# Two transformer blocks and a router: the second block's tiles cut across sequences, its attention moved to TensorE

## What is computed

```python
x  = x + xattn(layernorm(x), ctx)          # cross-attention, 16 heads of 32, 77 context rows per sequence, causal
h  = layernorm(x)                          # input of the second block, called with S = 8, B = 512
l1 = layer_norm(h) * ln1w + ln1b
q, k, v = split(l1 @ qkv_weight.T)         # 16 query heads, 4 key/value heads of 32
# einsum('bgqsd,bgtd->bgqst'): for each of the 512 positions, attention over the 8 SEQUENCES, causal in the sequence
h1 = h + attention(q, k, v) @ proj_weight.T
l2 = layer_norm(h1) * ln2w + ln2b
top 2 of 8 experts per token, 1,280 places per expert: gelu(l2 @ w1[e]) @ w2[e], weighted and added
out = x + h1 + moe
```

## Time and profile before

| | |
|---|---|
| median of 3 runs | 1815.31 us (1813.96 to 1817.59) |
| the profiled execution | 1818.26 us |
| its span, first to last instruction | 1816.5 us |
| mean granted TensorE clock | 0.911 |
| setup, to the last value of the cross-attention | 0 to 67.1 us |
| main stage | 67.1 to 979.8 us |
| routing, to the first expert transposes | 979.8 to 1053.4 us |
| experts | 1053.4 to 1816.5 us |

### The profile page before, as it was taken

One profiled execution on the slowest core, in us unless ns is written; L12 is line 12 of the kernel. 1 busy time (PEld: TensorE's weight loads), 2 busy tenths in 40 slices (PEclk: granted clock), 3 DMA queues, 4 the chain that ended last, 5 costly groups with the idle time before them and its releaser, 6 DMA issues. The chain is left out here.

```text
span 1816.5 us, 31665 instructions
## 1 busy us (share of the span) xinstructions
PE 1513.9 (83%) x10604; PEld 1324.4 (73%) x10605; DVE 1105.9 (61%) x1778; ACT 802.6 (44%) x2385; POOL 975.8 (54%) x925
## 2 busy tenths in 40 slices
PE   7778877799777988789752579999999979999986
PEld 5367766677666776677642478989999968999975
DVE  3256888967897798877866953544333374353361
ACT  2066654565555655457421043544333354343240
POOL 2014676756785677667884254655344385454342
PEclk9879997899898988889875789999999989999999
DMA  7101101111101111111001132433333352433221
GB/s 188 35 18 36 44 28 36 36 49 48 47 24 47 49 36 36 36 36 42 24 35 71 45 109 64 94 95 101 74 71 81 58 128 66 92 94 88 34 37 21
DMA packets 57936, 106.95 MB, mean 59 GB/s; under 512 B 14314, under 2 KB 14314, under 8 KB 57771
## 3 DMA queue, kind: packets, MB, share of 16 engines
q1 hardware_dynamic: 26707, 58.42, 10.1%
q0 software_dynamic: 17920, 29.08, 9.4%
q10 hardware_dynamic: 13144, 17.23, 2.7%
HBM read 79.83 MB, written 37.75 MB: 65 GB/s over the span
## 5 line engine op out<-in xcount | busy, mean ns | idle before, releaser
L1347 PE MATMUL hidden_ps<-gT,w 128*128 128x256 f32 x2880 | 351.8, 284 | 5.4 <-ACT hT L1269 2.5
L1347 PEld LDWEIGHTS hidden_ps<-gT,w 128*128 128x128 f32 x2880 | 349.4, 192 | 9.1 <-ACT hT L1269 5.2
L1376 PE MATMUL expert_ps<-w,hT 128*128 128x512 f32 x1440 | 340.2, 396 | 8.0 <-DVE og L1316 8.0
L1376 PEld LDWEIGHTS expert_ps<-w,hT 128*128 128x128 f32 x1440 | 272.1, 191 | 64.7 <-DVE og L1316 8.5
L1294 DVE TENSOR_TENSOR hT<-gl,hT 128x512 fp32r<-128x512 f32 x160 | 132.0, 834 | 246.9 <-ACT hT L1269 238.8
L1156 POOL TENSOR_TENSOR w<-raw,w 128x1024 fp32r<-128x1024 f32 x64 | 155.3, 2442 | 206.5 <-ACT w L1150 205.6
L1267 ACT ACTIVATE gl<-hidden_ps 128x512 f32<-128x512 f32 x160 | 95.8, 598 | 335.1 <-PE hidden_ps L1347 239.2
L1249 POOL DMA_INDIRECT out_dram<-og,idx x80 | 132.7, 1659 | 155.0 <-DVE og L1316 141.3
L452 POOL TENSOR_TENSOR prod_k<-qb,kc 128x128 f32<-128x128 f32 (+7 forms) x128 | 182.6, 1428 | 30.4 <-ACT vs L652 28.1
L626 ACT ACTIVATE pr<-score_ps,nm 128x77 f32<-128x77 f32 x512 | 158.7, 363 | 78.1 <-DVE nm L776 78.1
L469 POOL TENSOR_TENSOR prod_v<-pa,vc 128x128 f32<-128x128 f32 (+7 forms) x128 | 156.5, 1233 | 24.7 <-DVE ao L710 20.5
(11 more groups left out here) (186 smaller groups left out, 3352.7 us busy)
## 6 DMA issues: line engine op xcount, KB each, us to landing
raw<-L_ffn_moe_w_dram SPq DMA_DIRECT2D x64, 512.0 KB
xa<-x_dram SPq DMA_DIRECT2D x32, 256.0 KB, 2.8
xc<-x_dram SPq DMA_DIRECT2D x32, 256.0 KB, 2.7
out_dram<-x ACTq DMA_DIRECT2D x32, 256.0 KB, 2.0
normed_tokens<-z ACTq DMA_DIRECT2D x32, 256.0 KB, 2.3
xg<-normed_tokens,idx POOLq DMA_INDIRECT x80
out_dram<-og,idx POOLq DMA_INDIRECT x80
cx<-ctx_dram SPq DMA_DIRECT2D x1, 1232.0 KB
```

The lines of the kernel that those rows point to most:

```text
L1347: last = pe.matmul(pH[:, q, f * W:(f + 1) * W], w1[p][l][:, k, cols], xT[g.s % 2][r][:, k, :], start=k == 0 and n == 0, stop=k == KT - 1 a ...
L1376: last = pe.matmul(pY[:, k, :], hT[par][l][:, f, k * P:(k + 1) * P], w2[p][r][:, f, :], start=f == 0 and n == 0, stop=f == FT - 1 and n == 2)
```

## The change

It replaces the main stage; setup and routing follow from that.

- **Block one** keeps its tiles (one sequence, 128 positions). Its result x2 is now written to a DRAM tensor `mid`. The transposed shares come one step later (LP = 4). VectorE subtracts the maxima (two instructions of 616 columns), ScalarE does two exponentials of 616 columns, VectorE sums them, and GpSimd does the division.
- **Block two** works on other tiles: 16 positions of all 8 sequences, loaded from `mid` by four transfers of 32 tokens. Partitions 32j to 32j+31 hold 4 positions x 8 sequences, which is a closed block for the attention. It starts FF = 14 steps after block one's first tile, since its first tile needs all 8 sequences of a chunk.
- Its scores: VectorE turns q and k in blocks of 32 x 32 (`hq`, `kbd`), TensorE adds the mask by one matmul and does four 128 x 128 products (kind `s2`); VectorE takes maxima and subtracts, ScalarE one exponential of 512 columns, VectorE sums, GpSimd multiplies (`p2`), TensorE transposes (`p2t`) and does four products with the spread values `vbd` (`o2`); VectorE turns the result (`ao`).
- Everything is written out, 50 steps without a loop. Weights come already turned, constants come as inputs, and the routing has one more prefix matmul and one more sum because a tile holds 8 sequences.

```diff
-JOBS = [("pt", 3, 0), ("pt", 3, 1), ("xt", 1, 0), ("at", 7, 0), ("pt", 3, 2), ("pt", 3, 3), ("q", 2, 0), ("q", 2, 1),
-        ("z2t", 8, 0), ("zt", 4, 0), ("pj", 7, 0), ("pv", 3, 0), ("lg", 8, 0), ("qkv", 4, 0), ("qkv", 4, 1),
-        ("wo", 3, 0)]
+LP = 4
+FF = LP + 10
+STEPS = NT + FF + 4
...
+def ring_jobs(i):
+    tx, tq, tp = tile(i, 1), tile(i, 2), tile(i, LP)
+    fz, fs, fo, fr = (tile(i, FF + n) for n in range(4))
+    jobs = [("pt", tp, 0), ("pt", tp, 1), ("xt", tx, 0), ("pt", tp, 2), ("pt", tp, 3), ("zt", fz, 0), ("o2", fo, 0)]
+    if i % 2 == 0:
+        jobs += [("q", tq, 0), ("q", tq, 1)]
+    jobs += [("s2", fs, 0), ("pv", tp, 0), ("z2t", fr, 0), ("pj", fo, 0), ("p2t", fs, 0), ("qkv", fz, 0),
+             ("lg", fr, 0), ("qkv", fz, 1), ("wo", tp, 0)]
...
         @block.gpsimd
-                    pool.tensor_tensor(prod_k[:, g % 2, 0:n * P].rearrange("p (t h d) -> p t h d", t=n, h=HQ),
...
-                    pool.tensor_tensor(prod_v[:, g % 2, 0:n * P].rearrange("p (t h d) -> p t h d", t=n, h=HQ),
...
+                        pool.tensor_tensor(shares, shares, bc(rec[:, t % 2, 8 * half:8 * half + 8], 2, [P, 8, SK]),
+                                           ALU.mult).then_inc(s["shared"], 1)
...
+                    pool.tensor_tensor(vbd[:, f % 2, :, :, :],
+                                       bc(vn[:, f % 2, :].rearrange("p (g d) -> p g d", g=NKV), 2, shape),
+                    pool.tensor_tensor(p2[:, f % 2, :, :], p2[:, f % 2, :, :], bc(rec2[:, f % 2, :], 2, [P, 16, TB]),
+                                       ALU.mult).then_inc(s["shared2"], 1)
...
         @block.scalar
-                            e = act.activation(pr[:, b, g, :], psS[:, b, g * SK:(g + 1) * SK], ACT.Exp,
-                                               bias=nm[:, h:h + 1], scale=SCALE, accum_out=den[:, h:h + 1])
+                        act.activation(shares, shares, ACT.Exp, scale=SCALE).then_inc(s["exp_done"], 1)
+                    act.activation(p2[:, f % 2, :, :], p2[:, f % 2, :, :], ACT.Exp, scale=SCALE)\
...
         @block.vector
+                    dve.transpose(hq[:, :, :], parts(bank("qkv", f, 0))).then_inc(s["q_turned"], 1)
+                        k_turn = dve.transpose(kbd[rows, :, j, :],
...
+                    dve.transpose(ao[:, :], bank("o2", f)).then_inc(s["ao_done"], 1)
...
+                    chained(dve.tensor_reduce(nm2[:, :], scores, X, ALU.max, negate=True))
+                    dve.tensor_tensor(p2[:, f % 2, :, :], scores, bc(nm2[:, :], 2, [P, 16, TB]), ALU.add)\
...
+                        dve.tensor_tensor(pr[:, t % 2, 2 * half:2 * half + 2, :, :],
...
+                        chained(dve.tensor_reduce(den[:, heads], shares, X, ALU.add))
...
         @block.tensor
+                    pe.matmul(bank("s2", fs), token_sel[:, :], token_mask[:, :], start=True, stop=False)
+                    for g in range(NKV):
+                        last = pe.matmul(bank("s2", fs)[:, g * P:(g + 1) * P], hq[:, g, :],
+                                         kbd[:, g, :, :].rearrange("p j k -> p (j k)"),
...
+                        last = pe.matmul(bank("o2", fo)[:, g * P:(g + 1) * P], p2T[:, g, :],
+                                         vbd[:, fo % 2, g, :, :].rearrange("p j d -> p (j d)"), start=True, stop=True)
...
         @block.sync
+                    sp.dma_start(mid[row0(t):row0(t) + P, :], x2[:, t % 2, :]).then_inc(x2_out[t % 2], 16)
+                    for j in range(4):
+                        sp.dma_start(fx[TB * j:TB * (j + 1), f % FX, :], block_rows(mid, f, j))\
```

1085 lines of the change are left out of this document (524 added, 561 removed), and 3 rows, old and new, of the table read_out.

## The result

The changed kernel takes **1841.29 us** (median of 4 runs, 1839.02 to 1843.38), the kernel before 1816.45 in the same series. The ratio is 1.0138, 95% interval 1.0121 to 1.0156: slower, by 25 us. The forecast was 1846 us, +31 on 1815.

The account below looks back on a forecast made before the run. No main-stage engine was full; TensorE waited for VectorE's attention sums and x2. From 1818.3 us, main stage +32, setup -6, routing +5 gave 1849; the profiled execution being 3 above the median, 1846. Range for 8 in 10: 1785 to 1890.

Parts of the forecast that it names:

- port in single-block steps: Main stage, steps with one block alone: 4 us added for VectorE and GpSimd sharing a port.
- Joint steps: Steps with both blocks: 22.3 us odd, 27.3 even, plus 0.8 for clock and 0.4 for the port; steps 17 to 31 387.
- the 0.4 for the port: Joint steps: 0.4 us a step for VectorE's normings blocked by GpSimd, as most stand where VectorE has slack.
- Rival 1: Joint steps: TensorE alone sets them, 22.5 us instead of 25.9; 1765 in full, 1805 at half; chance 0.3.
- Rival 2: Single-block steps and behind transposes: lower clock slows queries and qkv, turning may take 1.44 us; 1890 and over; chance 0.1.
- Block one alone: Steps 4 to 13: output projection waits for oT_lo; 17.6 us even, 10.1 odd, plus 2.0 a step for lost clock.
- Block two alone: Steps 36 to 45: next step's input is late through GpSimd's chain, z2 and z; 16.2 us each, 162 in all.
- The shared port: VectorE's three normings a step: up to 1.27 us lost each by the skill's rule, 0.5 by the trace; 0.4 a step taken.
- My row: Trace of the kernel before: the same norming takes 539 ns, or 1,059 while GpSimd adds, a loss of 0.52 us.
- Turning: VectorE's 32 x 32 turning of 512 columns: no row had it, 0.65 us taken.
- Setup: Ahead of the main stage: keys start when Wk has landed, 13.1 us, and values follow at once; -6 us.
- Routing: After the last logits: waiting for six loads +3 us, one more prefix matmul and two small sums +2; +5 in all.

Follow-up runs that it names:

- experiment 4: Changed kernel with VectorE's norming z of the next tile moved ahead of the norming z2: 1815.94 us.
- Experiment 1: Changed kernel with block two's sums and reciprocals on VectorE moved ahead of block one's two subtractions and oT_lo: 1822.94 us.
- experiment 5: Changed kernel with three VectorE orders together: block two's sums earlier, oT_lo ahead of the scores' passes in steps 4 to 13, z ahead of z2: 1756.45 us.
- three_and_port: experiment 5 plus, on GpSimd, block one's division moved behind zT_lo and the addition to fx into the next step: 1754.31 us.
- Experiments 2 and 3: Changed kernel, steps 4 to 13: oT_lo ahead of block one's maxima, 1818.87 us; separately, ten overwritten matmuls in the pause before the output projection, 1823.69 us.
- experiment 8: three_and_port with GpSimd's addition behind the spread vbd, plus four overwritten matmuls before the output projection in steps 4 to 13: 1758.89 us.
- experiment 10: three_and_port with GpSimd's addition behind the spread vbd, plus block two's shares multiplied by the reciprocals on VectorE instead of GpSimd: 1765.50 us.

## Why the prediction was right

Each term of the main stage beside what it measured: the step ends are x2's starts, and behind step 35 the logits (36 to 45 counted from x2 of step 35; from its logits they are the 171.8 of experiment 4).

| | forecast | measured |
|---|---|---|
| start to end of step 4 | 60 | 59.0 |
| steps 5 to 9 | 83 | 81.8 |
| 10 to 13 | 63 | 65.0 |
| 14 to 16 | 68 | 69.2 |
| 17 to 31 | 387 | 378.9 |
| 32 to 35 | 90 | 92.6 |
| 36 to 45 | 162 | 167.5 |
| last four | 28 | 26.6 |
| port in single-block steps | 4 | in the rows above |
| main stage | 945 (+32) | 940.5 (+27.8) |
| setup | -6 | -10.8 |
| routing | +5 | +6.1 |
| experts | 0 | +2.0 |

- **Joint steps.** The pause ahead of the shares' transposes was forecast at 2.6 (odd) and 2.0 us (even); it is 2.96 and 1.55. Experiment 1 shows its cause, the place of the sums on VectorE. The mean step is 25.26 us where 25.8 were counted. The schedule itself, 22.3 and 27.3 us, came out as 22.5 and 26.9 in the one pair at a clock of 1.00, and the clock cost the other pairs 1.5 us, 0.8 a step as counted (0.97 granted in steps 17 to 31). What does not show is the 0.4 for the port. What the prediction did not have is the second wait behind the first: taking the pause away alone wins 0.2 us a pair at equal clock, and 2.7 with z moved too (experiment 5).
- **Rival 1** set TensorE's own joint step at 22.5 us. With most waits taken away (three_and_port) it is 46.1 / 2 = 23.05, and without the 1.6 us of idle that TensorE still has in such a pair I estimate 22.3. So the rival named the floor, and the forecast the obstacle in front of it. **Rival 2** did not come: turning takes 0.70 us, not 1.44, and the queries kept the 2.4 GHz level (0.29 us a matmul of 256 columns on average).
- **Block one alone.** The pause for oT_lo is there, 4.2 to 4.8 us in steps 5 to 9 and 2.7 to 3.3 in 10 to 13, and behind it the output projection is at the 1.2 GHz level in part or whole, 4.4 to 5.5 us instead of 3.0: 1.4 to 2.5 a step, where I had added 2.0. Experiments 2 and 3 show them to be two costs, worth 16.7 and 13.4 us in steps 4 to 13. They do not add up: behind the better order the dummies lost time (experiment 8).
- **Block two alone.** The mechanism was right, the size short by 5 us: z behind z2 behind GpSimd's five and two small instructions, but the two normings take 1.49 and 1.30 us where I had about 0.55 for z and only 1.2 of blocking. The clock is in it too: three steps at 1.00 take 16.4 us, where 16.2 were counted, and six others, all but one at 0.80 to 0.91, take 17.0 to 18.5.
- **The shared port.** I chose the smaller price, 0.5 us for one norming and 0.4 a step. Here z2 and z lose 0.95 and 0.90 us each and aT_lo 0.67, 2.5 us of VectorE in a joint step. My row has 0.52. When they start, 1.21, 1.16 and 0.80 us of GpSimd's instruction are left, so they lose 0.1 to 0.3 us less than that. This is nearer to the rule of the Trainium skill, "SBUF — State Buffer", "Who interferes with whom", that the loser is blocked for the whole of the other's instruction, than to my row. The section of the Trainium skill also says that an instruction of VectorE with two inputs from SBUF contends with GpSimd's reads, and that one with at most one does not, unless it runs in a two-port mode, which tensor_scalar can enter. The trace agrees: `aT_lo`, with both inputs in SBUF, takes 1.36 us, `xT_lo` and `oT_lo`, the same operation with one input from PSUM, 0.69 and 0.68, and the two normings, tensor_scalar with one tensor read from SBUF, are stretched. That they run in such a mode no row here shows.
- **Turning** 512 columns takes 0.70 to 0.72 us, where 0.65 was taken out of bounds of 0.54 and 1.44.
- **Setup.** The step that failed is the landing of Wk, taken over from the earlier trace rows: the load of the weight turned on the host takes 7.9 us, not 11.8, so the keys start at 9.24, not 13.1. The small loads land at 25.9 us, earlier than the 32 that I had kept.

```profile
rk<-wk_rows_dram SPq DMA_DIRECT2D x1, 1024.0 KB, 7.9
...
9.24 19.56 PE L272 MATMUL setup_ps<-cT,rk 128*128 128x308 f32 x64 [9.24 <-DMA rk<-wk_rows_dram]
...
25.87 3.66 DVE L251 TENSOR_SCALAR kT<-setup_ps,bk 128x308 f32<-128x308 f32 x8 [25.87 <-DMA wr<-router_rows_dram]
```

- **Routing.** The first instruction comes 6.8 us after the last logits (996.8) instead of 1.9, +4.9 where +3 was said, since SP issues the six loads only at 999.59, behind the last stores:

```profile
999.59 0.34 SPq L866 DMA_DIRECT2D ranks<-expert_ranks_dram  x1
...
1003.56 0.42 DVE L891 TENSOR_REDUCE best<-logits 128x32 f32<-128x256 f32 x1 [11.44 <-DMA number<-token_numbers_dram]
```

Errors of both signs partly cancelled, and that is luck: steps 17 to 31 were put 8 us too long, 36 to 45 5 too short, the setup 5 too long. What was not tried: the six loads issued ahead of the last stores; oT_lo ahead of block two's sums in the joint steps, which experiment 10 points to; the old tiles of block two with the new setup, which would tell what the attention by matmuls is worth by itself; and a better order of VectorE in the kernel before, so that the gain below compares a reordered kernel with one that was not.

So the expected gain was there: the change took 199 us off GpSimd and 77 off VectorE. It turned into new waits, at three places of one engine's order. With these alone moved the same work takes 1756 us, with two passes of GpSimd moved too 1754 or 1752 by their place, which the runs do not tell apart: 3.4% less than the kernel before.
